# One plan for the first expert stage, its norms and the first attention

## What is computed

```python
def _moe_forward(x, Wg, W_in, W_out):          # layer 0's ffn: 8 experts, top 2, capacity
    xf = x.reshape(-1, h)
    probs = jax.nn.softmax(xf @ Wg, axis=-1)
    top_vals, top_idx = jax.lax.top_k(probs, K)
    ...
    hid = jnp.einsum('ech,ehf->ecf', inp, W_in)
    a, g = jnp.split(hid, 2, axis=-1)
    out_e = jnp.einsum('ecf,efh->ech', jax.nn.gelu(a, approximate=False) * g, W_out)
    ...
    y = (gathered * gates[..., None]).sum(axis=1)

def _L0_attn_ref(x, W_Q, W_K, W_V, W_O):       # 16 heads of 8, causal, bias by distance
    attn = jnp.einsum('bhqd,bhkd->bhqk', Q, K) / jnp.sqrt(jnp.float32(HD))
    attn = jnp.where(causal[None, None], attn + bias[None], -jnp.inf)
    attn = jax.nn.softmax(attn, axis=-1)
    out = jnp.einsum('bhqk,bhkd->bhqd', attn, V)
```

## Time and profile before

| | us |
|---|---|
| runs shown: median, lowest, highest | 1519.11, 1517.02, 1519.50 |
| the profiled execution | 1519.04 |
| its span, first to last instruction | 1517.1 |
| mean granted clock of TensorE over the span | 0.953 |

### The profile page before, as it was taken

One profiled execution on the slowest core, in us unless ns is written; L12 is line 12 of the kernel. 1 busy time (PEld: TensorE's weight loads), 2 busy tenths in 40 slices (PEclk: granted clock), 3 DMA queues, 4 the chain that ended last, 5 costly groups with the idle time before them and its releaser, 6 DMA issues.

```text
span 1517.1 us, 27015 instructions
## 1 busy us (share of the span) xinstructions
PE 1358.6 (90%) x10934; PEld 571.3 (38%) x10934; DVE 1001.6 (66%) x1517; ACT 884.7 (58%) x1112; POOL 403.6 (27%) x331
## 2 busy tenths in 40 slices
PE   4999977888887899998999998999889999999997
PEld 2544432333333344443333433334333343334342
DVE  4333348888862545677887677686887788586735
ACT  2322333677786365254656558886678865665572
POOL 5365500010101466552222203112213032112000
PEclk8799986999998899998999999999899999999999
DMA  5632001100000632110101101102001001101100
GB/s 163 113 56 56 1 16 38 38 2 2 2 2 0 136 84 59 29 30 12 36 11 21 22 1 22 23 1 54 0 1 22 15 19 22 29 1 30 22 1 14
DMA packets 30279, 45.80 MB, mean 30 GB/s; under 512 B 5886, under 2 KB 10686, under 8 KB 30110
## 3 DMA queue, kind: packets, MB, share of 16 engines
q1 hardware_dynamic: 30156, 44.08, 13.5%
HBM read 25.39 MB, written 1.18 MB: 18 GB/s over the span
## 4 chain that ended last, share of the span: by engine, by line
PE 73%; ACT 10%; DVE 9%; issue 6%; POOL 1%; SPq 1%; DMA 0%; POOLq 0%; ACTq 0%; DVEq 0%
PE ps L1291 14%; PE ps L1337 12%; ACT PR L1369 6%; PE ps L1277 5%; PE ps L1643 4%; PE ps L1079 3%; PE ps L1644 3%; PE ps L1645 3%; PE ps L1669 3%; DVE BM L1403 2%; PE ps L1757 2%; PE ps L1269 2%; PE ps L1093 2%; PE ps L1094 2%; PE ps L1095 2%
## 5 line engine op out<-in xcount | busy, mean ns | idle before, releaser
L1369 ACT ACTIVATE PR<-ps 128x1024 f32<-128x1024 f32 x432 | 433.6, 1024 | 247.5 <-PE ps L1298 144.6
L1403 DVE TENSOR_REDUCE BM<-ps 128x2 f32<-128x1024 f32 (+2 forms) x384 | 348.4, 949 | 54.5 <-PE ps L1277 53.5
L1291 PE MATMUL ps<-QS,KS 48*128 48x512 f16 (+7 forms) x2688 | 307.0, 330 | 44.4 <-ACT PR L1369 35.2
L1337 PE MATMUL ps<-PR,VS 128*32 128x512 f32 (+3 forms) x2304 | 237.7, 505 | 3.3 <-ACT PR L1369 2.8
L1277 PE MATMUL ps<-KS,QS 48*128 48x128 f16 (+2 forms) x1728 | 168.1, 282 | 29.8 <-DVE BM L1403 19.7
L1291 PEld LDWEIGHTS ps<-QS,KS 48*128 48x128 f16 (+1 forms) x2688 | 107.2, 95 | 218.5 <-ACT PR L1369 104.1
L1396 DVE TENSOR_REDUCE BM<-ps 128x8 f32<-128x1024 f32 x96 | 116.7, 1219 | 42.6 <-PE ps L1277 42.2
L1277 PEld LDWEIGHTS ps<-KS,QS 48*128 48x128 f16 x1728 | 69.9, 96 | 158.2 <-DVE BM L1403 69.1
L1071 POOL TENSOR_TENSOR HL<-HL,PR 128x512 f32<-128x512 f32 x64 | 82.7, 1293 | 84.1 <-ACT HL L1117 83.2
L1147 DVE SCALAR_TENSOR_TENSOR HL<-ps,HL 128x512 f32<-128x512 f32 x64 | 44.2, 691 | 87.0 <-POOL HL L1071 87.0
L2282 POOL TENSOR_TENSOR KS<-BT,HL 128x1024 f16<-128x1024 f32 x14 | 33.1, 2368 | 228.3 <-DMA QS<-KS 207.2
(11 more groups left out here) (306 smaller groups left out, 2193.5 us busy)
## 6 DMA issues: line engine op xcount, KB each, us to landing
PR<-gates SPq DMA_DIRECT2D x32, 512.0 KB, 13.9
QS<-KS SPq DMA_DIRECT2D x64, 128.0 KB
QS<-KS SPq DMA_DIRECT2D x64, 64.0 KB
WM<-W_in SPq DMA_DIRECT2D x1, 2048.0 KB, 9.3
QS<-HL SPq DMA_DIRECT2D x48, 32.0 KB
KS<-HL SPq DMA_DIRECT2D x48, 32.0 KB
QS<-CT SPq DMA_DIRECT2D x96, 2.0 KB
KS<-KS SPq DMA_DIRECT2D x8, 128.0 KB, 2.4
```

The source lines that it names most:

```text
L1291: ins = pe.matmul(ps[pair][:, w, off:off + cols], KS[rows, ks, kt * P:(kt + 1) * P], QS[rows, qs, (ph + 1) * TT - cols:(ph + 1) * TT], sta ...
L1337: ins = pe.matmul(dst[32 * j:32 * j + 32, TT - cols:TT], v, PR[:, buf, j, off:off + cols], start=(g == 0), stop=(g == NGRP[ph] - 1))
L1369: act.activation(dst, src, ACT.Exp, scale=0.125 if lat else 1.0).then_inc(sig["exp"], 1)
L1403: ins = dve.tensor_reduce(BM[:, ph, p, :, qt - 4 * ph, part], bnk[:, :, off:off + nk * P], AX.X, ALU.max)
```

## The change

The hand-written expert stage and norms 1 and 2 go away. Their tasks enter `First`, which now plans the experts, norm 1 by batch, the projections by batch, the 8 quads and norm 2 by batch as one. The functions `experts` and `norm` move from `Late` up to `Plan`, and the code that emits these tasks moves from `pe_late` and its fellows into `pe_attn` and its fellows, which both plans use. `Late` keeps its ranks and costs.

- An expert unit now multiplies both halves on DVE first and the gate on POOL after, in a ring of 8 buffers that lie in `OS`, `ON`, `RX` and two pieces of `HL`; the gelu's ring lies in `BT`.
- The split weights lie in head slots 8 to 15 of `QS`, the split inputs in two-tile rings in the second half of `YA`. POOL clears slots 0 to 7 in their stead, and the constant rows of slots 0 to 7 are loaded at the start, those of 8 to 15 after the last expert unit, ahead of the stack of quad 4.
- New waits: exps of the first four groups wait until the gates they overwrite are used (`et` 47 or 63), the first product with the values waits for the last expert update, and the stack of quad 4 for the last expert unit.
- Norm 1 of batch 0 needs only tiles 0 and 1 of the experts; norm 2 of batch 0 needs only quads 0 to 3. Router 1 still reads all four tiles.

```diff
+    NHE = 8
+    table = "exp"
...
-    ORDER = {"ACT": ("qkh", "ev", "vc", "ln", "exp", "rx"),
-             "DVE": ("ct", "m4", "den", "qkl", "add", "red"),
-             "POOL": ("vs", "on"),
-             "SP": ("crow", "put")}
+    ORDER = {"ACT": ("exh", "ewh", "eg", "qkh", "vc", "ev", "sq", "vln", "vex", "ln", "exp", "rx"),
+             "DVE": ("exl", "ewl", "eup", "eh", "ct", "m4", "den", "cen", "scl", "qkl", "add", "red"),
+             "POOL": ("et", "vs", "on"),
+             "SP": ("egb", "crow", "put")}
...
+    def norm(self, kn, b):
+        add = self.add
+        for t in (2 * b, 2 * b + 1):
+            src = {1: ("eup", t), 2: ("add", NQ * b + 3, t % 2), 3: ("eup", t) if b == 0 else ("eu", 63), 4: ("add", NQ * b + 3, t % 2), 5: ("mup", 2, t),
+                   6: ("oup", t), 7: ("fup", t), 8: ("add", NN + NQ * b + 3, t % 2)}[kn]
+            fused = kn in (3, 5, 7)
+            if kn not in (4, 8):
+                m = add("PE", f"mean{b}", ("mean", kn, t), src, ("eup", t) if kn == 3 else None)
+                src = add("DVE", f"cen{b}", ("cen", kn, t), m)
+                self.take(m, "misc", src)
+            sq = add("ACT", f"sq{b}", ("sq", kn, t), src)
+            v = add("PE", f"var{b}", ("var", kn, t), sq)
+            ln = add("ACT", f"vln{b}", ("vln", kn, t), v)
+            self.take(v, "misc", ln)
+            x = add("ACT", f"vex{b}", ("vex", kn, t), ln)
+            done = scl = add("DVE", f"scl{b}", ("scl", kn, t), x)
+            if kn in (5, 6):
+                add("DVE", f"scb{b}", ("scb", kn, t), scl)
+            if fused:
+                x = add("ACT", f"ve0{b}", ("ve0", kn, t), ln)
+                done = add("POOL", f"ff{b}", ("ff", kn, t), x, scl)
+            self.take(sq, "nr", scl, done)
...
+        if kind == "eu":
+            return 1.2 + sum(1 for x in self.held.values() if x[0] == "eu") * 0.3
...
-            v = None if units >= 2 or lead > 4 else (1.9 if lead <= 2 else 2.1) + units
+            v = None if units >= 2 or lead > 4 else (1.9 if lead <= 2 else 2.1) + units - (self.at["eu"][1] < 63)
...
-            v = {"turn": 0, "qk": 1, "val": 1.9, "proj": 2.7}[kind]
+            v = {"turn": 0, "qk": 1, "val": 1.9, "proj": 2.7, "ed": 1.1, "mean": 1, "var": 1}[kind]
+            if kind in ("ed", "mean", "var"):
+                return v
...
+    def experts(self):
+        add = self.add
+        for t in range(NT):
+            for g in range(4):
+                add("SP", "egb", ("egb", t, g), ("et", 16 * t - 17) if t >= 2 else None)
+            x = add("ACT", "exh", ("exh", t), ("eu", 16 * t - 9) if t >= 1 else None)
+            add("DVE", "exl", ("exl", t), x, ("eu", 16 * t - 17) if t >= 2 else None)
+        for c in range(E):
+            x = add("ACT", "ewh", ("ewh", c), ("eu", 2 * c - 4) if c >= 2 else None)
+            add("DVE", "ewl", ("ewl", c), x)
+        for u in range(64):
+            t, i = divmod(u, 16)
+            q = add("PE", "eu", ("eu", u), ("exl", t), ("ewl", min(u // 2, 7)))
+            x = add("ACT", "eg", ("eg", u), q, ("eh", u - 3) if u >= 3 else None)
+            x = add("DVE", "eh", ("eh", u), x, ("ed", u - self.NHE) if u >= self.NHE else None)
+            self.take(q, "pair", x)
+            x = add("POOL", "et", ("et", u), x, ("egb", t, i // 4))
+            x = add("PE", "ed", ("ed", u), x)
+            if i == 15:
+                self.take(("ed", u - 15), "misc", add("DVE", "eup", ("eup", t), x))
...
+        self.experts()
+        for b in range(B):
+            self.norm(1, b)
+            self.prologue(b)
+            for n in range(b * NQ, b * NQ + NQ):
+                self.quad(n, [("put", n)], [("vs", n), ("eup", NT - 1) if n == 0 else None])
+                self.add("POOL", "vs", ("vs", n), ("vc", b), ("pv", n - 2, 1, NGRP[1] - 1) if n >= 2 else None)
+            self.norm(2, b)
+
+    def prologue(self, b):
...
+        for w in range(2):
+            q = add("PE", f"pre{b}", ("qk", b, w), ("scl", 1, 2 * b), ("scl", 1, 2 * b + 1))
+            h = add("ACT", f"pre{b}", ("qkh", b, w), q)
+            self.take(q, "pair", h, add("DVE", f"pre{b}", ("qkl", b, w), h))
...
-        def pe_norm(pe, k, ready):
+        def pe_norm(pe):
...
+        def egb_value(lat, t):
+            return 16 * (2 * lat + t // 2 + 1)
...
+            if kind == "eu":
+                u, = args
+                t, i = divmod(u, 16)
+                e, ch = divmod(i, 2)
+                if i == 0:
+                    pe.wait_ge(sig["exl"], c("exl", t))
+                if t == 0:
+                    pe.wait_ge(sig["ewl"], c("ewl", e))
+                for g in range(2):
+                    f = slice(g * F0 + ch * P, g * F0 + (ch + 1) * P)
+                    ins = three(pe, ps[slot][:, g, :], (WIH1[:, e, f], WIL1[:, e, f]), (XHR[:, t % 2, :], XLR[:, t % 2, :]))
+                ins.then_inc(sig["eu"], 1)
+            elif kind == "ed":
+                u, = args
+                t, i = divmod(u, 16)
+                pe.wait_ge(sig["et"], c("et", u))
+                pe.matmul(single(plan, ("ed", 16 * t)), w_out[:, i // 2, i % 2, :], ring_he(lat, u), start=(i == 0),
+                          stop=(i == 15)).then_inc(sig["ed"], 1)
+            elif kind == "mean":
...
+        def norm_mode(kn):
+            return {1: "plain", 2: "plain", 3: "fused", 4: "rms", 5: "fused", 6: "ln2", 7: "fused", 8: "rms"}[kn]
+
+        def nr1(plan, kn, t):
+            i = plan.slot[("sq", kn, t)]
+            if kn < 3:
+                return HLw[:, 1024 * i + 512 * (2 - kn):1024 * i + 512 * (3 - kn)]
+            return VSf[:, 512 * (i + 1):512 * (i + 2)]
+
+        def ring_eg(lat, u):
+            return GE0[:, u % 3, :] if lat else BT[:, u % 3, :]
+
+        def ring_he(lat, u):
+            i = u % plan_of(lat).NHE
+            if lat and i < NHF:
+                return HF[:, i, :]
+            i -= NHF * lat
+            if i < 6:
+                return (OS, ON, RX)[i // 2][:, i % 2 * TT:(i % 2 + 1) * TT]
+            return HLw[:, 1024 * (i - 4) + 512:1024 * (i - 4) + 1024]
...
+                    elif n == NQ:
+                        pe.wait_ge(s_cdma2, 32)
...
+                        if n == 0:
+                            pe.wait_ge(sig["eup"], c("eup", NT - 1))
...
-                elif lat:
+                else:
...
+        def pool_attn(pool, lat, c, plan, task):
+            if task[0] == "et":
+                u, = task[1:]
+                t, i = divmod(u, 16)
+                pool.wait_ge(s_egb[t % 2][i // 4], egb_value(lat, t))
+                pool.wait_ge(sig["eh"], c("eh", u))
+                pool.tensor_tensor(ring_he(lat, u), ring_he(lat, u), GB[:, t % 2, i // 2, :], ALU.mult).then_inc(sig["et"], 1)
+                return
...
+        def sp_egb(sp, lat, c, t, g):
+            sp.wait_ge(s_gw, 16 * (lat + 1))
+            if t >= 2:
+                sp.wait_ge(sig["et"], c("et", 16 * t - 17))
+            src = gate_d[lat, 2 * g:2 * g + 2, t * TT:(t + 1) * TT].unsqueeze(0)
+            sp.dma_start(GB[:, t % 2, 2 * g:2 * g + 2, :], src.to_broadcast([P, 2, TT])).then_inc(s_egb[t % 2][g], 16)
...
-            for h in range(8, H):
+            for h in range(8):
...
+                sp.dma_start(QS[64 * w + 24:64 * w + 24 + SLOPE_PIECES, 0:8, :], a["slopes"][w][:, 0:8, :]).then_inc(s_cdma, 16)
...
-            sp.wait_ge(s_out, NT * 2 * E)
-            for w in range(2):
-                sp.dma_start(QS[64 * w + 24:64 * w + 24 + SLOPE_PIECES, :, :], a["slopes"][w]).then_inc(s_cdma, 16)
+            sp.wait_ge(s_hg, 1)
+            sp.dma_start(gate_d[0].rearrange("e (i t) -> (e i) t", t=P), gT[:, :]).then_inc(s_gw, 16)
...
+                    if m == NQ:
+                        sp.wait_ge(sig["eu"], c("eu", 63))
+                        for w in range(2):
+                            sp.dma_start(QS[64 * w + 24:64 * w + 24 + SLOPE_PIECES, 8:H, :],
+                                         a["slopes"][w][:, 8:H, :]).then_inc(s_cdma2, 16)
...
-            act_norm(act, 0)
+            act_norm(act)
             act_router(act, 0)
             act_comp(act)
-            act_moe(act)
-            act_norm(act, 1)
             act_first(act)
-            act_norm(act, 2)
             act_decay(act, ch)
             act_router(act, 1)
...
-            pe_norm(pe, 0, (s_xup, 4))
+            pe_norm(pe)
             pe.wait_ge(s_w, N_WFIRST)
-            pe_router(pe, 0, 0, w_rt0[:, :])
+            pe_router(pe, 0, w_rt0[:, :], range(1, NT + 1))
             pe_comp(pe)
-            pe.wait_ge(s_compd, 2)
-            pe_moe(pe)
-            pe_norm(pe, 1, (s_xup, 8))
-            pe_first(pe, 1)
-            pe_norm(pe, 2, (s_xup, 12))
-            pe_router(pe, 1, 2, w_rt0[:, :])
+            pe_first(pe)
+            pe_router(pe, 1, w_rt0[:, :], [counter(False)("scl", 2, t) for t in range(NT)])
             pe_late(pe)
```

562 lines of the change are left out of this document (178 added, 384 removed), and 2 rows, old and new, of the table COST.

## The result

The changed kernel takes **1483.94 us** in the median of 4 runs (1481.38 to 1484.72), the kernel before 1518.66 beside it. The ratio is 0.977, 95% interval 0.9753 to 0.9787. The profiled execution took 1484.72, its span is 1483.0, its mean clock 0.969. The forecast was 1487.4, its range 1472 to 1504.

A forecast was written before the change was run, and what follows sets the result against it. PE was taken to fill the expert stage, leaving the idle of 191 to 292 us to take. 210 + 40 + 172.4 + 9.4 + 8 + 3 + 3 + 6.2 = 452.0 for router 1, 31.6 less: 1487.4 us, range 1472 to 1504.

The forecast's parts named there:

- Start of router 1: Router behind the first attention and second norm: forecast to start at 452.0 us, against 483.6 before.
- first 28 exps: Start of the first attention: 40 us forecast, floor 33 at ACT's pace, ceiling 44 at the steady pace.
- Expert stage: First expert stage: takes in norm work, projections and 17 units, first unit at 157, ends at 210 (bounds 206 and 213).
- Work moved into the attention: Batch 1's norm and projections and batch 0's second norm inside the attention: 8 us, bounds 0 and 12.
- Lead of the units: Last quads of the attention: DVE's shorter lead over the end costs 3 us, bounds 0 and 10.3.
- Clock: PE's granted clock dips after the expert stage, costing 3 us, bounds 0 and 7.
- Second norm: Behind the last add: only tile 3's chain is left, 6.2 us to router 1 against 9.4 before.
- After router 1: Router 1 and everything later: order kept, 0 us of change, the same 1035 us.
- A: Rival: batch 1's work all hidden in PE's idle, first exps at ACT's pace, no clock dip; 1468 us, chance 0.17.
- B: Rival: in the attention the vector engine takes the place of the waits, no lead; 1507 us, chance 0.18.
- C: Rival: batch 0's stack is late, few units done when the experts end, first exp waits 13 us; 1496 us, chance 0.07.
- D: Rival: slower, PE's short waits between groups let the clock fall and stay down; 1530 us, chance 0.08.

The follow-up runs named there:

- e12_again: The kernel after run once more, unchanged; 1484.92 us, ratio 0.9793.
- e2_tail: The kernel after with norm 2 of batch 0 held back until the last add, behind the attention; 1483.19 us, ratio 0.9772.
- e10_pe: The kernel after with only PE's instructions of batch 1's norm 1 and projections doubled; 1488.94 us, ratio 0.982.
- e5b_units: The kernel after with the favour for attention units during the expert stage taken away, in the first plan only; 1500.52 us, ratio 0.9893.
- e7_twice: The kernel after with batch 1's norm 1 and projections issued twice on PE, DVE and ACT; 1494.08 us, ratio 0.9863.
- e1_serial: The kernel after with norm 1's means waiting for the last expert tile, so without the overlap; 1522.8 us, ratio 1.0042.
- e8_warm: e4_comp with unused products of zeros in PE's setup waits, ahead of transposes, means and router 0; 1470.54 us, ratio 0.9696.
- e9_warm2: e8_warm with 18 more unused wide products among the small products of router 0 and of the weights; 1476.33 us, ratio 0.9743.
- e11_rest: The kernel after with batch 1's norm 1 and projections doubled on DVE and ACT, not on PE; 1488.32 us, ratio 0.9818.
- e3_fill: The kernel before with 24 unused products put into PE's 5.9 us wait for the first stack; 1512.62 us, ratio 0.9977.
- e4_comp: The kernel after with the 32 small products of layer 1's weights moved into PE's waits inside router 0; 1476.51 us, ratio 0.9724.

## Why the forecast held, and where it was off

*What bounds the kernel.* Right. The experts pay for everything that is put among them (165.24 of 165.30), and the idle of 191 to 292 is what could be taken.

*Start of router 1.* Forecast 452.0, measured 451.8, by errors that cancel:

```
term                                   forecast   measured
setup                                  +0         +3.1 (scatter, e12_again)
first exp at                           210        215.8
first 28 exps, batch 1's work in them  40 + 8     47.6
other 116 exps                         172.4 + 3  175.4
clock                                  3          0 up to 440
last exp to router 1                   15.6       12.9
router 1 to the second expert stage    0          -1.4
```

*Expert stage.* Mechanism right, size off: 24 units, not 17. They came every 2.7 us, as forecast, the first at 154 rather than 157, but they went on to the end of the stage at 218.1, where I had stopped them at 203 of 210. The setup is 3.1 of these 8.1 us. The stage itself took 165.4 us instead of 160.4, of which seven units more are 3.5; the rest I can't itemise. The first unit was early because the chain ahead of it was shorter than forecast: the mean of tile 1 stood at 128.44 (forecast 124), its norm took 6.5 us (scaling 134.94) and not the 11 of the earlier trace rows, and from there to the first transfer of the stack 7.7 us (142.64) and not 11. The first exp did not wait for the last expert step, as I had it, but went 2 us ahead of it, so it is 5.8 late and not 8.1.

*Work moved into the attention.* I had 8 us for batch 1's norm and projections and batch 0's second norm together. The doubled work prices the first at 8.5 in the 28 exps, and e2_tail the second at 3.1 in the other 116: 11.6 in place of 8, near the bound of 12 that I had called the case of nothing hidden. My reason (PE and DVE near their limit) holds for PE: in e10_pe the price is PE's busy time. The 28 exps without batch 1's work are then 47.6 - 8.5 = 39.1, for my 40. This takes the price of a second copy for that of the first.

*Lead of the units.* This is the term that was mis-sized, though the sum doesn't show it. I gave a shorter lead 3 us of loss in the last quads. There is none: without batch 0's norm (e2_tail) the 116 exps took 172.3 us, no more than the 173.0 of the kernel before, and with hardly a unit done in the expert stage (e5b_units) only 0.6 more than in the kernel after. In the last quads DVE did 8.94 of 31 us, more than in the earlier trace rows but still mostly idle. The 3 us too much here and the 3.6 too little in the term above cancel, which is luck. What the forecast had no term for is how much the lead is worth at the front: 22 us by the marks, 17 by the medians, about half of the change, 21 of the 22 up to the 28th exp.

*Clock.* No dip where I had put it: 1.00 in the mean from 60 to 440, and 0.86 in 440 to 452, some 3 us at the lower level, which are within the 12.9 of the next term. Forecast 3, rivals up to 7. By the Trainium skill (TensorE: Matmul & The Clock Gate, section "A second HAM failure mode: psum-queue depth-cycling") the mix of groups on three pairs of banks could have let it oscillate; the trace disagrees, PE was busy 83 to 90% in the stretches from 218 to 440 and the clock stayed up.

*Second norm.* The size was near (12.9 from the last exp to router 1 for 15.6), the mechanism wrong. I had left one tile's norm behind the last add and let router 1 wait for it. Rows of DVE in the kernel after, the last add and the last two scalings:

```profile
447.33 0.69 DVE L1442 TENSOR_TENSOR XT<-XT,ps 128x512 f32<-128x512 f32 x1 [1.03 <-PE ps L1277]
...
452.26 0.69 DVE L1393 TENSOR_TENSOR XN<-XN,HL 128x512 f32<-128x512 f32 x1 [2.27 <-ACT HL L1321]
453.50 0.69 DVE L1393 TENSOR_TENSOR XN<-XN,HL 128x512 f32<-128x512 f32 x1 [0.55 <-ACT HL L1321]
```

Both of batch 1's tiles are scaled after the last add, and router 1 starts ahead of both, at 451.79: it takes its tiles in order and waits for each by itself, and batch 0's two were ready. From the end of the last add to router 1 it is 3.8 us for the forecast's 6.2. And e2_tail shows that batch 0's norm is paid inside the attention nearly in full; as a part of the change it is nothing.

*After router 1.* I had it unchanged; to the end of the span it took 1031.2 in place of 1033.5. 1.4 of it are router 1's 32 products, 3.63 us at full clock where before they ran 5.09.

*Rivals.* A fell with e7_twice; B with the 116 exps at 175.4 in place of its 182.7 (DVE is at 47.71 of 57 in the middle, 84%); C with the first unit at 154; D with the clock rows. e1_serial shows D's sign by another mechanism: the same tasks without the overlap are slower than before.

## What to carry over

When a stage that fills one engine is followed by one in which that engine waits for others, move the others' work forward by letting the full engine issue the small products that feed them, and give these the higher rank; without that rank, merging two plans brought half. Look for errors that cancel even when the total is right: two terms here were off by 3 us and more in opposite directions. Price the moved work at PE's full time where it goes, and more where it makes PE wait, and ask of each part whether only its place has changed. When a stage has been packed, look next at what stands between two stages: here the waits of the setup gave 13 us, more than a third of what the large change gave.

## What the runs showed of the hardware

- PE's granted clock fell to 0.50 in e8_warm at 24.8 us, with PE busy 4.00 of 4 us in 24 to 28, in products of 8 and of 32 columns; in e9_warm2, with 10 wide products among them, it fell at 30.2.
- In e11_rest the same 473 products took 47.09 us at a mean clock of 0.91 and 43.21 at 1.00 in the kernel after: 3.9 us for the lower clock.
- The clock row reads 1.00 in 14 to 18 us in both profiles of the kernel after, while the same eight mean products took 6.07 us in one and 3.70 in the other. What the row does not tell there stays open.
- Filling a wait to hold the clock paid where the chain that follows is PE's own (setup, 6 us), and not where PE then waits for others (e3_fill 2 us at most by its profile, e9_warm2 a loss).
- POOL's first product, released by the gates' landing, starts 6.0 to 6.2 us behind the first expert product in e4_comp, e8_warm and e9_warm2. Full pace of PE ahead of it bought nothing (e9_warm2).
- SP issued the stacks at 0.7 us a transfer, 36 in a row in e1_serial, and a row that was ready stood 11 us behind the last 16 of them.
